# Sixteen counting matmuls moved behind the sums of gathered rows in a layer-0 tile

## The reference, cut to what matters

```
# layer 0
msg = edge_weight[:, None] * x[src]
agg = segment_sum(msg, dst, N)
h   = relu((x + agg) @ W1 + b1);   x = layernorm(x + h @ W2 + b2)
# layer 1
f   = softplus(edge_attr @ nn_w1.T + nn_b1) - log 2        # first filter layer
W   = (softplus(f @ nn_w2.T + nn_b2) - log 2) * c[:, None]
agg = segment_sum(W * h1[edge_index[1]], edge_index[0], N) # h1 = x @ lin1_w.T
x   = layernorm(x + (h1 + agg) @ lin2_w.T + lin2_b)
```

## Time and profile before

| | us |
|---|---|
| median of the runs (2 runs, 8995.32 to 8999.62) | 8997.47 |
| the profiled execution | 9018.67 |
| its span, first to last instruction | 9016.8 |
| gathers of layer 0 (L499), first start to last start | 72.3 to 4331.1 |
| mean granted TensorE clock | 0.743 |

### The profile page before, as it was taken

The page is one execution under the profiler, slowest core; times in us unless marked ns, Lnnn a source line. Parts: engine busy times, 40 slices in busy tenths (PEclk is TensorE's granted clock), DMA queues, the critical chain, the costliest instruction groups (busy, mean ns, idle before and its releaser), DMA issues. The chain is left out here.

```text
span 9016.8 us, 199238 instructions
## 1 busy us (share of the span) xinstructions
PE 5937.2 (66%) x35386; PEld 4768.7 (53%) x35658; DVE 5857.1 (65%) x17865; ACT 3463.0 (38%) x6782; POOL 6200.3 (69%) x6552
## 2 busy tenths in 40 slices
PE   4666666666666666666655555767666676676687
PEld 3444444444444444444444444666666666666676
DVE  6666666666666665555655555777777777777776
ACT  3333333333333333333544443344434443334302
POOL 5777767777777767777167777777777777777720
PEclk7777767667677766676855556888888888888897
DMA  5444444444444444444444445666666666666676
GB/s 155 145 146 144 146 140 146 145 146 145 144 146 146 144 141 147 144 147 144 145 136 135 133 133 156 216 213 214 213 212 217 213 213 214 212 212 215 213 238 206
DMA packets 805241, 1537.36 MB, mean 171 GB/s; under 512 B 193150, under 2 KB 206900, under 8 KB 804707
## 3 DMA queue, kind: packets, MB, share of 16 engines
q1 hardware_dynamic: 595415, 1097.64, 37.8%
q0 software_dynamic: 209456, 436.16, 16.5%
q10 hardware_dynamic: 348, 3.33, 0.1%
HBM read 971.97 MB, written 564.58 MB: 170 GB/s over the span
## 5 line engine op out<-in xcount | busy, mean ns | idle before, releaser
L499 POOL DMA_INDIRECT xg<-x_rows,gidx x3224 | 3046.0, 945 | 1266.1 <-issue 925.8
L1317 POOL DMA_INDIRECT sorted_messages<-rows,sidx x3224 | 3110.6, 965 | 1156.0 <-issue 947.4
L551 PE MATMUL bank<-onehot,xg 128*128 128x42 f32 x6448 | 1106.2, 324 | 1409.7 <-DMA xg<-x_rows,gidx 1399.9
L551 PEld LDWEIGHTS bank<-onehot,xg 128*128 128x128 f32 x6448 | 993.2, 230 | 1483.4 <-DMA xg<-x_rows,gidx 1471.5
L561 PE MATMUL bank<-attr,nn 128*128 128x512 f32 x1612 | 1459.8, 1060 | 1.2 <-DVE hid L585 0.8
L1245 PE MATMUL bank<-hot,block_rows 128*128 128x128 f32 x8256 | 1388.9, 344 | 32.4 <-DVE hot L1399 32.3
L1245 PEld LDWEIGHTS bank<-hot,block_rows 128*128 128x128 f32 x8256 | 1341.1, 257 | 58.4 <-issue 20.3
L1215 PE MATMUL bank<-w_nn2T,e_hid 128*128 128x128 f32 x6448 | 1042.1, 314 | 308.9 <-DMA e_hid<-hidden 301.1
L1215 PEld LDWEIGHTS bank<-w_nn2T,e_hid 128*128 128x128 f32 x6448 | 1008.9, 226 | 265.8 <-DMA e_hid<-hidden 233.1
L1226 PE MATMUL bank<-h1w,ohT 128*128 128x128 bf16 x3224 | 333.1, 266 | 970.4 <-DVE ohT L1346 970.4
L1370 DVE SCALAR_TENSOR_TENSOR rows<-filt,meta,bank 128x128 f32<-128x128 f32 x3224 | 904.8, 343 | 103.5 <-DVE filt L1361 68.5
(11 more groups left out here) (220 smaller groups left out, 7860.8 us busy)
## 6 DMA issues: line engine op xcount, KB each, us to landing
block_rows<-sorted_messages SPq DMA_DIRECT2D x346, 792.0 KB
hidden<-hid SPq DMA_DIRECT2D x404, 512.0 KB
e_hid<-hidden SPq DMA_DIRECT2D x403, 512.0 KB
sorted_messages<-zero SPq DMA_DIRECT2D x403, 264.0 KB
dstb<-dst SPq DMA_DIRECT2D x403, 256.0 KB
attr<-attr_cols SPq DMA_DIRECT2D x403, 204.0 KB
xg<-x_rows,gidx POOLq DMA_INDIRECT x3224
sorted_messages<-rows,sidx POOLq DMA_INDIRECT x3224
```

What stands on the lines that cost most here:

```text
L499: pool.indirect_dma_start(xg[s][:, :], None, x_rows, bass.IndirectOffsetOnAxis(ap=gidx[s // HALF][:, s % HALF:s % HALF + 1], axis=0),).the ...
L551: nc.tensor.matmul(bank[0][:, 0:WIN], xg[s][:, :], onehot[:, s, :], start=(s == 0), stop=(s == SUB - 1)).then_inc(summed, 1)
L1317: pool.indirect_dma_start(table, bass.IndirectOffsetOnAxis(ap=sidx[b][h][:, s:s + 1], axis=0), rows[b][h][:, s, :], None).then_inc(landed[ ...
```

## The change

The 16 counting matmuls, with their two waits and their increment of `counted`, stand behind the loop over windows (the sums) in PE's stream, and ahead of L556 and L561. No other stream is changed, and no operation is added or removed.

```diff
                             with pe.Fori(first, past_last) as t:
                                 windows = jobs.windows()
-                                pe.wait_ge(oha_set, t + 1)
-                                pe.wait_ge(seen_set, t + 1)
-                                for s in range(SUB):
-                                    nc.tensor.matmul(above, lower[:, :], oha[:, s, :], start=(s == 0), stop=(s == SUB - 1))
-                                for s in range(SUB):
-                                    ins = nc.tensor.matmul(in_tile, ones16[:, :], oha[:, s, :], start=(s == 0), stop=(s == SUB - 1))
-                                ins.then_inc(counted, 1)
                                 with pe.Fori(0, windows):
...
                                     jobs.step()
+                                pe.wait_ge(oha_set, t + 1)
+                                pe.wait_ge(seen_set, t + 1)
+                                for s in range(SUB):
+                                    nc.tensor.matmul(above, lower[:, :], oha[:, s, :], start=(s == 0), stop=(s == SUB - 1))
+                                for s in range(SUB):
+                                    ins = nc.tensor.matmul(in_tile, ones16[:, :], oha[:, s, :], start=(s == 0), stop=(s == SUB - 1))
+                                ins.then_inc(counted, 1)
                                 if q + 1 < PARTS:
                                     pe.wait_ge(digits_set, t * 2 + 2)
```

## The result

| | before | changed |
|---|---|---|
| median of the runs, us | 8997.47 | 10,232.57 (10,227.29 and 10,237.85) |
| ratio, 95% interval | | 1.1375, 1.1346 to 1.1403 |
| the profiled execution, us | 9018.67 | 10,227.29 |
| gathers of layer 0, first to last start | 72.3 to 4331.1 | 74.2 to 5544.3 |
| one tile there | 10.57 | 13.58 |

The direction was forecast, the size was not: 9920, range 9785 to 10,130. The whole difference is in the loop that was touched: its gathers span 5470.1 us in place of 4258.8, 1211.3 more, and the profiled execution got 1208.6 longer. The rest of the kernel takes the time that it took.

What follows compares the result with a forecast made beforehand. Layer 0 was taken to be bound by a two-tile loop through POOL, landing, PE and ACT. Adding 303 x 2.36 + 100 x 2.10 = 925 us to the median 8997.47 gave 9922, stated as 9920, range 9785 to 10,130.

Steps and rivals of the forecast that it cites:

- The bound: Layer 0's edge loop: a two-tile chain through POOL, landing, PE and ACT, 20.70 us for two tiles, sets the pace.
- The counting was hidden before: Layer 0, PE: the counting, 0.89 us, lay outside the two-tile loop, hidden by the wait for gathers 5 to 7.
- DVE's work behind the counting is the larger part: L561 waits for DVE's `hid` or digits behind the counting: L668 to the end of L684, 3.62 us, joins the loop.
- The sum: Landing to L561: 4.72 us more for two tiles, 4.21 in the last part; 925 us over all tiles.
- the counting at the high clock: PE's 16 counting matmuls take 0.89 us, since L561 and the sums, some 6 us of busy PE, run ahead.
- the time from the landing to the counting: From the start of ACT's `gidx[1]` copy to the first matmul behind the sums: 0.54 us.
- the loop of one tile: Through PE and DVE, L561 to L561: 10.19 us, shorter than 12.9, only limits how far two tiles drift apart.
- unknown terms, landing and clock: Gather 7's landing kept at 3.97 us (ends -135 and +322 us); counting's clock kept high (low level +131 us).
- E: Rival: layer 0's landings line up badly behind the `hid` store and `attr` load, 5.6 us each tile: 10,244 us; chance 0.05.
- A: Rival: PE's clock is low throughout, so the counting takes 1.54 us: 10,053 us; chance 0.15.

Runs made afterwards that it cites:

- 4: Kernel before, with ACT's copy of the next tile's `gidx[0]` moved between the softplus of half 0 and half 1: 8945.97 us, ratio 0.9932.
- 7: Changed kernel, with ACT's copy of the next tile's first row indices moved between the two halves' softplus: 9739.82 us.
- 6: Kernel before, with 16 elements of `attr` loaded a tile in place of the whole load (output not the reference's): 8817.55 us.
- 9: Kernel before, with the load of `attr` in two halves, each as soon as L561 has read that half: 8821.55 us, ratio 0.9804.
- 12: Kernel before, with each of the 16 counting matmuls made twice: 8956.62 us, against 8994.31 beside it.
- 3: Changed kernel, with DVE's `hid` of both halves and the digits put ahead of its wait for `counted`: 9314.09 us.
- 1: Changed kernel, with `attr` loaded whole once and only 16 elements a tile in the loop (output not the reference's): 9733.65 us.
- 2: Changed kernel, with 32 extra matmuls on PE behind the counting, ahead of its wait for DVE, into an unread bank: 10,001.10 us.
- 13: Changed kernel, with the load of `attr` in two halves, each as soon as L561 has read that half: 10,241.54 us.

## Why the prediction was wrong in size and right in direction

- **The bound** (a loop of two tiles through POOL, landing, L561, softplus and ACT): right. Taking ACT's link out shortened both kernels (4 and 7), taking the landing's delay out brought the kernel before to POOL's pace (6, 9). That it was only 0.35 to 0.57 us above that pace was right too: 9.99 in the median.
- **The counting was hidden before**: right (12).
- **DVE's work behind the counting is the larger part**: right. From L668 to L561 it is 3.88 us in the median tile, where the forecast had 3.87 in the parts with digits. Taking it out gave 4.5 for two tiles (3), the pairs included. PE's waits for `low` came in 303 tiles, as forecast.
- **The sum.** For two tiles the kernel before has, as means over the tiles, 8.82 to gather 7, 3.91 for the landing, 0.85 to L561, 2.09, 4.20 and 1.22 back to gather 0. The changed kernel has 8.80, 4.01, 6.87, 2.09, 4.19 and 1.18. So all that was added, 6.0 us, is in the way from landing to L561, where the forecast added 4.72, and 4.21 in the last part: 4.59 on average. That is the mis-sized term, by 1.43. Half of it times 403 tiles is 288 us, and the profiled execution missed its forecast by 10,227 - 9944 = 283. From 9920 to the median of 10,232 it is 312, since the profiled execution lies 21 us above the median before and 5 below it now. (The forecast counted the landing from ACT's copy, 0.19 behind the landing itself, which moves that much from one term to the other.)
- **What it is made of.** The forecast took the counting at the high clock, 0.89. It takes 1.35 on average: 0.46 of the 1.43. It is 1.54, the low level, in all 202 long tiles and in some four of ten short ones. I had argued that L561 and the sums run ahead of it, but in the long tile PE waits for rows in between. The other 1.0 us is the time from the landing to the counting, 1.69 on average, for 0.54 + 0.19 = 0.73 in the forecast's rows. It is 0.88 in the long tiles and 2.52 in the short ones, where PE is still busy with the sums.
- **The step that failed.** The forecast worked out the loop of one tile, 10.19 us, saw that it was shorter than 12.9 and wrote that it only limits how far two tiles can drift apart. It didn't ask what happens when they do, and kept both of its unknown terms, landing and clock, at one value for all tiles. The tiles do drift apart. The short tile then runs at that loop's pace (10.0 to 12.3), where a quick landing, 3.23, is of no use, for PE isn't free. The long tile carries its whole chain, with gather 7 issued 3.8 to 6.1 us behind L561 (10th to 90th percentile), beside the load of `attr`: 4.77 for the landing. A mean landing of 4.01 looks as forecast, but the pair pays the long tile's: 8.80 + 4.77 + 6.23 + 2.09 + 4.19 + 1.18 = 27.3 us, and twice 13.58 is 27.2. Against 21.1 + 4.59 = 25.7 the long tile has 0.86 more in the landing and 0.65 more in the counting at the low clock. Without the load the landings are even (2.64), the pairs nearly vanish, and 24.7 = 2 x 12.36 (1).
- **Rivals E and A.** E (landings of 5.6 in each tile) gave 10,244 and had 0.05. That its number is so close is luck: the long tiles' landings are late, but by less, and the low clock of A is in every long tile as well. The range should have reached up to it, since the forecast itself named the new place of gather 7 and then let it be.
- **What stays open.** What the low clock in the counting costs alone (2 didn't hold it), and whether the changed kernel's long landings come of the load's time or its bytes (13 didn't move it far enough). That the long tile's chain sets the pair fits its terms, and the pairs go where the load (1) or DVE's stretch (3) goes; why the tiles settle in pairs is argued, not shown.

The Trainium skill (DMA: Bandwidth & Descriptors, "Issuing engines are not separate DMA queues") says that transfers issued by different engines run on the same DMA engines and interleave. The trace agrees: beside SP's load of 204 KB POOL's gather 7 lands in 3.64 us in the median, without it in 2.54 (1).

## What to carry to other kernels

Before moving work on one engine, write down everything that waits for its result and is itself waited for by what comes next: here the 0.9 us of moved matmuls pulled 3.9 us of DVE's work in with it. When a loop over two iterations is the bound, work out both the mean and the two tiles of a pair; where they may drift apart, the pair pays the worse tile's landing, and the other's slack is lost. And a transfer's landing is a term with a place in time: two half loads, each issued as soon as its half is free, gave 2% in the kernel before with the same bytes, and nothing in the changed one, where SP's earlier stores held them back.

## What the hardware showed that I had not expected

- Gather 7 (128 rows of 512 bytes) lands 2.5 us after its issue in the median with no `attr` load in the loop (1, 6). With one it takes 3.6 in the changed kernel and 5.9 or more in a tenth of the tiles, while the sixteen DMA engines are busy for only 0.36 of the loop. The place in the tile counts without that load too: gathers 1 and 2 take 3.4 and 3.2 in run 6.
- L561 starts at the low clock in nearly every tile of both kernels, 2.09 us to the softplus; 32 matmuls into an unused bank bring that to 1.16 and the changed kernel 231 us down (10,232 to 10,001).
- Doubling the counting in the kernel before didn't cost anything (8957, one run), with the granted clock at 0.775 in place of 0.743.
